# One late block of a factorisation-machine tower added on VectorE before the last layer-1 product, its sums copied earlier, and other shares for the last two steps

## The chip, the cores and the metric

The kernel runs on one core of one Trainium2 chip. The metric is the device time of one execution in microseconds (us), the median of the runs. One core has five engines with queues of their own: TensorE (PE in the profile, with PEld for its weight loads), VectorE (DVE), ScalarE (ACT), GpSimd (POOL) and SyncE (SP), which here only issues DMAs. They are held in step by semaphores: an instruction waits until a counter that others raise has reached a number.

## The reference, cut to what matters

```python
e = stack([tbl_f[ids[:, f]] for f in range(32)], axis=1)     # 2048 x 32 x 64, fp32
p, q = e[:, ROW_IDX], e[:, COL_IDX]                          # the 496 pairs of 32 fields
z = einsum('bne,hne,bnh->bn', p, kernel, q)                  # 2048 x 496
h = concatenate([z, dense_ctx], axis=1)                      # 2048 x 512
h = maximum(h @ W_top1 + b_top1, 0.0)                        # 512
h = maximum(h @ W_top2 + b_top2, 0.0)                        # 256
y = h @ W_top3                                               # 2048 x 1
```

## The kernel before

The batch of 2048 is cut into 8 pairs (`PAIRS`) of two times 128 rows, and each pair goes through 64 steps (`NS`), 512 steps (`STEPS`) in all. A step computes the products of one half slot, up to 16 field pairs for 128 rows (upright steps) or for 256 (turned steps): TensorE multiplies embeddings by the pair matrices into a ring of three PSUM tiles `T` (lines 730 and 742), and VectorE multiplies the result by the other embeddings (lines 586 and 604 to 612). For a turned step TensorE then sums over the partitions with a matrix of ones into `psZ` (line 767), several steps to a burst. For an upright step the 16 sums over 64 elements are divided: the first `share(n)` columns are summed by VectorE (line 633, with one instruction for two steps where that is possible) and the others by ScalarE, one column per instruction pair (line 523, an activation with an accumulator and the read of the accumulator). These sums land in `z` and are transposed on TensorE into the same `psZ` (line 681). Then ScalarE copies `psZ` to `zT` (line 510, `evacuate_z`, two of the four blocks of 128 features at once), and the dense layers run on it between the steps of the next pair.

The order on every engine is written out in advance by tables of steps. The last pair has no next pair, so its layers run in a tail after step 511. The change is in this tail and in the two steps ahead of it. In the kernel before:

- The last two steps, 510 and 511 (n = 62 and 63 of the last pair), are upright; `DVE_SHARE` gives VectorE 11 of the 16 columns of each and ScalarE 5. Their columns belong to the fourth block of z (k = 3) and so do those of a few steps before.
- ScalarE makes the sums of step 510, then the last copy of `psZ` (`evacuate_z(PASSES - 1)`, at `STEPS - 2`, line 510: blocks k = 2 and 3), and then the sums of step 511. The copy holds block 2 whole, but of block 3 only the sums of the turned steps: the upright sums are not ready when it is made.
- TensorE (lines 790 to 813) multiplies blocks 0 and 1 by W1 for the four groups m of 128 outputs (line 788), waits for the copy (`z_block_out`), multiplies blocks 2 and 3 of the copy, waits for all sums (`mult_done`, `dve_reduced`, `act_reduced`), and transposes the upright part of block 3 to PSUM (`LAST_Z`, line 808).
- ScalarE copies `LAST_Z` to `late` in SBUF (line 565). TensorE waits for that (`tail_act` 1), and multiplies `late` by the same weights of block 3 (line 812). So block 3 is multiplied twice, once for each part.
- The layer-1 results are added to the bias and cut at zero by ScalarE for m = 0 and 2 (line 568) and by VectorE for m = 1 and 3 (line 652), layer 2 follows (line 819), then its two ReLUs (lines 570 and 652), layer 3 (line 691), a copy to `y` (line 573) and the store (line 405).

An fp32 product of 128x128 weights with 256 columns is two matmul instructions in the profile.

Of the kernel before, what the change touches and what calls it, by code (L numbers as in the profile page):

```python
# [46 lines left out]
HALVED = (10, 14, 15, 16, 17, 19)  # L47
HALVED_FROM = 2
HALVED_LAST = (1, 2, 3, 5, 6, 7, 9, 10, 12, 15, 16, 17)
K_LEAD = 3  # L50
TR_STEP = (-12, -9, -1, 0, 6, 16, 29, 30)
TR_OUT = ((-15, 6), (-15, 6), (-4, 1), (-3, 5), (5, 2), (13, 3), (23, 8), (23, 8))
# [90 lines left out]
def dlrm_tower(nc, dense, ids, tables, W1, b1, W2, b2, W3, KT, out):  # L143
# [157 lines left out]
    with ctx:  # L301
# [54 lines left out]
        tail_dve = sem("tail_dve")  # L356
        y_out = [sem(f"y_out{u}") for u in range(2)]

        def share(n):

            return DVE_SHARE[ORDERED[n][0]]

        def embeddings(t, b, g):
            rows = slice(GF * (g % 2), GF * (g % 2) + GF)
# [4 lines left out]
        LAST_Z, L1_OUT = ends[4], (psE[:, 0:2 * P], ends[1], ends[2], ends[3])  # L369
        L2_OUT, L3_OUT = (ends[5], psZ[:, 0:2 * P]), ends[0]  # L370
        LAST_ZT = (PAIRS - 1) % 2
        late = zT[:, 1 - LAST_ZT, 0, :]

        FREE_AT = {}
        for t in range(1, PAIRS):
# [17 lines left out]
        @block.sync  # L393
        def _(sp):
            def load_k(s):
                sp.dma_start(kst[:, k_cols(s)], KT[:, k_cols(s)]).then_inc(k_in[s], 16)

            def load_dense(t):
                for b in (0, 1):
                    to = z[:, b, :].rearrange("p (b c) -> p b c", c=P)[:, :, P - DC // KC:P]  # L400
                    sp.dma_start(to, dense[bass.ts(2 * t + b, P), :].rearrange("p (b c) -> p b c", b=KC)).then_inc(dense_in, 16)

            def store_y(t):
                to = out[:, 2 * P * t:2 * P * (t + 1)].rearrange("o (q b) -> (o q) b", q=QUADS)
                sp.dma_start(to, y[0:P:QUAD, t % 2, :]).then_inc(y_out[t % 2], 16)

            sp.dma_start(idx[:, 0, :], ids[0:P, :]).then_inc(idx_first, 16)
            sp.dma_start(idx[:, 1, :], ids[P:2 * P, :]).then_inc(idx_second, 16)
            ready = {x: m for m, x in enumerate((x, b) for some, bs in UNITS[0] for x in some for b in bs)}
            loads = []  # L410
            for n in FIRST:
                s, x = ORDERED[n][0], max(ready[x] for part in stacks_of(n) for x in part)
                if s not in [load for load, _ in loads]:
                    loads.append((s, x))
            behind = {m: x for x, m in ready.items()}
            held = -1
            for m, (s, x) in enumerate(loads):
                if x - 2 * K_LEAD > held and x >= 2 * GS:
                    held = max(1, x - 2 * K_LEAD)
                    x, b = behind[held]  # L420
                    sp.wait_ge(gathered_0[b][x], 16 * 2)
                load_k(s)
                if m == 9:
                    sp.dma_start(idx[:, 2:2 * PAIRS, :], ids[2 * P:B, :].rearrange("(t p) f -> p t f", p=P)).then_inc(idx_rest, 16)
            sp.wait_ge(z_zero, 1)
            load_dense(0)
            some, bs = UNITS[0][-1]
            sp.wait_ge(gathered_0[bs[-1]][some[-1]], 16 * 2)
            sp.dma_start(w1[:, :, :], W1.rearrange("(k p) m -> p k m", p=P)).then_inc(weights_in, 16)
            sp.dma_start(w2[:, :, :], W2.rearrange("(k p) m -> p k m", p=P)).then_inc(weights_in, 16)  # L430
            sp.dma_start(w3[:, :], W3).then_inc(weights_in, 16)
            sp.dma_start(b1c[:, :], b1).then_inc(weights_in, 16)
            sp.dma_start(b2c[:, :], b2).then_inc(weights_in, 16)
            for t in range(PAIRS):
                if t > 0:
                    sp.wait_ge(bank_free, ordinal["l3", t - 1, 0] + 1)
                    store_y(t - 1)
                if t < PAIRS - 1:
                    sp.wait_ge(summed, 2 * bursts * (t + 1))
                    load_dense(t + 1)  # L440
            sp.wait_ge(tail_act, 5)
            store_y(PAIRS - 1)
            for u in range(2):
                sp.wait_ge(y_out[u], 16 * (PAIRS // 2))

        @block.gpsimd
        def _(pool):
            def gather(t, g, b, f):
                f += GF * g
                nc.gpsimd.indirect_dma_start(  # L450
                    out=embeddings(t, b, g)[:, f % GF, :], out_offset=None, in_=tables[f],
                    in_offset=bass.IndirectOffsetOnAxis(ap=idx[:, 2 * t + b, f:f + 1].bitcast(U32), axis=0),
                ).then_inc(gathered[b][g] if t else gathered_0[b][f // 2], 16)

            def halve(t, some):

                k, ring = share(some[0]), upright_at[t, some[0]] % SHARED_RING
                pool.wait_ge(mult_done, when(t, some[-1]) + 1)
                p = prod[:, ring:ring + len(some), 0:k * D].rearrange("p x (n h) -> p x n h", h=D)
                nc.gpsimd.tensor_tensor(p[:, :, :, 0:D // 2], p[:, :, :, 0:D // 2], p[:, :, :, D // 2:D], ALU.add).then_inc(half_done, 1)  # L460

            nc.gpsimd.memset(ident[:, :], 0.0).then_inc(ident_0, 1)
            pool.wait_ge(idx_first, 16)
            for m, (some, bs) in enumerate(UNITS[0]):
                for x in some:
                    for b in bs:
                        for f in (2 * x, 2 * x + 1):
                            gather(0, f // GF, b, f % GF)
                if m == 0:
                    assert bs == (0,)  # L470
                    pool.wait_ge(ident_0, 1)
                    nc.gpsimd.affine_select(out=ident[:, :], in_=ident[:, :], compare_op=ALU.not_equal, fill=1.0,
                                            base=0, pattern=[[-1, P]], channel_multiplier=1).then_inc(ident_1, 1)
                    pool.wait_ge(idx_second, 16)
            pool.wait_ge(idx_rest, 16)
            for t in range(PAIRS):
                for n in range(NS + 1):
                    if n < NS and GATHERS[t][n]:
                        if NS * t + n > 0:
                            pool.wait_ge(mult_done, NS * t + n)  # L480
                        gather(*GATHERS[t][n])
                    for some in REDUCES[t]:
                        if WHEN[t][some[-1]] == n - 1 and some[-1] in halved(t):
                            halve(t, some)

        @block.scalar
        def _(act):
# [24 lines left out]
            def reduce(t, n):  # L512
# [3 lines left out]
                    act.wait_ge(z_zero, 1)  # L516
                if (t, n) in FREE_AT:
                    act.wait_ge(summed, bursts * (2 * t - 1 + FREE_AT[t, n]))
                for k, m in enumerate(range(share(n), SIZE[s])):
                    if k > 0:  # L520
                        outs(when(t, n), k)
                    x = place(t, n)[:, m * D:(m + 1) * D]
                    last = nc.scalar.activation(x, x, ACT.Copy, accum_out=z[:, b, Z_COLUMNS[s][m]:Z_COLUMNS[s][m] + 1])  # L523
# [29 lines left out]
            for at in range(STEPS):  # L553
                t, n = at // NS, SEQ[at // NS][at % NS]
                outs(at, 0)
                if (t, n) in upright_at:
                    reduce(t, n)
                for m in range(1, 16):
                    outs(at, m)
                if at == STEPS - 2:  # L560
                    evacuate_z(PASSES - 1)
            assert not outs_at

            act.wait_ge(tail_pe, 1)
            nc.scalar.activation(late, LAST_Z, ACT.Copy).then_inc(tail_act, 1)
            for m in (0, 2):
                act.wait_ge(tail_pe, 2 + m)
                nc.scalar.activation(h1T[:, m, :], L1_OUT[m], ACT.Relu, bias=b1c[:, m:m + 1]).then_inc(tail_act, 1)
# [7 lines left out]
        def _(dve):  # L576
# [37 lines left out]
                last.then_inc(mult_done, 1)  # L614

            def reduce(t, some):
                k = share(some[0])
                ats = []
                for n in some:
                    s, b = ORDERED[n]  # L620
                    assert share(n) == k and Z_COLUMNS[s][:k] == list(range(Z_COLUMNS[s][0], Z_COLUMNS[s][0] + k))
                    ats.append(b * KC * P + Z_COLUMNS[s][0])
                by = ats[-1] - ats[0] if len(some) > 1 else P
                assert by != 0
# [26 lines left out]
            def relu(o, x, bias):  # L651
                nc.vector.tensor_scalar(o, x, bias, 0.0, ALU.add, ALU.max).then_inc(tail_dve, 1)

            for m in (1, 3):
                dve.wait_ge(tail_pe, 2 + m)
                relu(h1T[:, m, :], L1_OUT[m], b1c[:, m:m + 1])
# [4 lines left out]
        def _(pe):  # L661
# [137 lines left out]
                    last_l1(m, k, zT[:, LAST_ZT, k, :])  # L799
            pe.wait_ge(z_block_out, PASSES)  # L800
            for m in range(M1):
                for k in range(2, KC):
                    last_l1(m, k, zT[:, LAST_ZT, k, :])
            pe.wait_ge(mult_done, STEPS)
            pe.wait_ge(dve_reduced, reduces_of(NU * PAIRS))
            pe.wait_ge(act_reduced, NU * PAIRS)
            for b in (0, 1):
                last = nc.tensor.transpose(LAST_Z[:, b * P:(b + 1) * P], z[:, b, (KC - 1) * P:KC * P], ident[:, :])
            last.then_inc(tail_pe, 1)
            pe.wait_ge(tail_act, 1)  # L810
            for m in range(M1):
                last_l1(m, KC - 1, late).then_inc(tail_pe, 1)
            for k in range(M1):
                if k % 2:
                    pe.wait_ge(tail_dve, k // 2 + 1)
                else:
                    pe.wait_ge(tail_act, 2 + k // 2)
                for m in range(M2):
                    last = nc.tensor.matmul(L2_OUT[m], w2[:, k, m * P:(m + 1) * P], h1T[:, k, :], start=(k == 0), stop=(k == M1 - 1))
                    if k == M1 - 1:  # L820
                        last.then_inc(tail_pe, 1)
            for k in range(M2):
                if k:
                    pe.wait_ge(tail_dve, 3)
                else:
                    pe.wait_ge(tail_act, 4)
                for q in range(QUADS):
                    last = last_layer(L3_OUT, k, q)
            last.then_inc(tail_pe, 1)
# [43 lines left out]
```

## Time and profile before

| | us |
|---|---|
| median of 3 runs | 777.03 (776.97 to 777.16) |
| profiled execution, its own time | 776.94 |
| its span, first to last instruction | 775.0 |
| PE busy | 737.8 (95%) |
| DVE busy | 712.9 (92%) |
| ACT busy | 677.7 (87%) |
| POOL busy | 539.3 (70%) |

The rows are read like this: a start in us from the start of the span, a busy time in us, the engine, the line of the kernel, the operation, what it writes and reads, and how many instructions are merged in the row. A bracket behind a row is idle time of that engine just before it, with what ended it. Neighbouring instructions of one engine overlap a little in these rows, so the spacing of the starts, and not the duration, is what one more instruction costs in a full queue.

### The profile page before, as it was taken

Reading aid. Unit: us, or ns where it says so; the run is one execution under the profiler, and the core shown is the slowest. Engines: PE = TensorE matmul, PEld = TensorE weight load, DVE = VectorE, ACT = ScalarE, POOL = GpSimd, SP = SyncE. Lnnn points to the kernel's source line nnn. Section 1 sums busy time; section 2 is a strip of 40 time slices with the busy share of each in tenths; the row PEclk is TensorE's granted clock in tenths of the full one; section 3 lists DMA queues with packets and bytes.
Section 4 is the critical chain, followed back from the end, with each engine's and each line's share of the span. In section 5 each row is a group of like instructions: output and inputs, shape, how many; then the busy total and the mean of one; then the engine's idle time right before and its main releaser. Section 6 shows DMA issues by size and latency. Waiting matters only on the chain.

```text
span 775.0 us, 18419 instructions
## 1 busy us (share of the span) xinstructions
PE 737.8 (95%) x5448; PEld 447.9 (58%) x5448; DVE 712.9 (92%) x698; ACT 677.7 (87%) x5274; POOL 539.3 (70%) x560
## 2 busy tenths in 40 slices
PE   4589999899999999999999999999999999999998
PEld 1354545556546666666655666566756666556645
DVE  0679988989999999999999999999999999989993
ACT  1678986788898899998999999998999989998984
POOL 6777777777766678877787778877787777882110
PEclk9989999999999999999999999999999999999999
DMA  3345411111111111111111111111101111010000
GB/s 122 93 134 155 143 28 28 28 27 29 25 26 22 25 25 23 25 27 25 27 22 27 28 25 24 24 28 27 26 22 27 28 26 25 22 24 3 1 1 1
DMA packets 33187, 28.08 MB, mean 36 GB/s; under 512 B 19776, under 2 KB 20800, under 8 KB 33088
## 3 DMA queue, kind: packets, MB, share of 16 engines
q0 software_dynamic: 16384, 16.81, 9.7%
q1 hardware_dynamic: 16704, 10.11, 4.8%
q8 instruction: 43, 0.70, 0.4%
q14 instruction: 56, 0.46, 0.2%
HBM read 26.87 MB, written 0.01 MB: 35 GB/s over the span
## 4 chain that ended last, share of the span: by engine, by line
PE 79%; ACT 9%; DVE 5%; issue 4%; POOL 3%; DMA 0%; DVEq 0%; POOLq 0%
PE T L742 31%; PE T L730 19%; PE psZ L767 11%; PE psE L686 10%; ACT prod L523 7%; PE psE L671 4%; POOL E_low L450 3%; DVE prod L604 1%; DVE prod_t L586 1%; PE psZ L681 1%; ACT eT L494 1%; DVE z L633 1%; PE T L788 1%; DVE prod L607 0%; DVE prod L612 0%
## 5 line engine op out<-in xcount | busy, mean ns | idle before, releaser
L523 ACT ACTIVATE prod<-prod 128x64 f32<-128x64 f32 x2560 | 612.0, 246 | 14.6 <-DVE prod L604 6.1
L523 ACT ACTIVATION_READ_ACCUMULATOR prod<-prod 128x1 f32 x2560 | 493.9, 193 | 0.0
L742 PE MATMUL T<-kst,eT 64*128 64x512 f32 (+3 forms) x2304 | 329.8, 418 | 11.5 <-ACT eT L494 4.3
L450 POOL DMA_INDIRECT E_low<-tbl,idx x256 | 241.7, 944 | 86.3 <-issue 60.1
L450 POOL DMA_INDIRECT E_high<-tbl,idx x256 | 241.9, 945 | 81.7 <-issue 60.1
L604 DVE TENSOR_TENSOR prod<-T,E_low 128x1024 f32<-128x1024 f32 x192 | 229.6, 1215 | 27.4 <-DMA E_low<-tbl,idx 22.2
L586 DVE TENSOR_TENSOR prod_t<-T,eT 128x1024 f32<-128x1024 f32 x192 | 231.7, 1215 | 12.5 <-PE psZ L767 5.6
L742 PEld LDWEIGHTS T<-kst,eT 64*128 64x128 f32 x2304 | 178.6, 190 | 93.0 <-issue 41.2
L730 PE MATMUL T<-eT,kst 64*128 64x256 f32 x1536 | 202.7, 388 | 4.3 <-issue 1.7
L730 PEld LDWEIGHTS T<-eT,kst 64*128 64x128 f32 x1536 | 141.3, 187 | 78.1 <-issue 32.8
L633 DVE TENSOR_REDUCE z<-prod 128x16 f32<-128x1024 f32 (+18 forms) x179 | 154.2, 871 | 1.0 <-POOL prod L460 1.0
L494 ACT ACTIVATE eT<-psE 128x512 f32<-128x512 f32 (+2 forms) x83 | 41.0, 494 | 70.6 <-PE psE L671 70.4
L767 PE MATMUL psZ<-prod_t,ones 128*32 128x512 f32 x768 | 100.7, 597 | 0.0
L460 POOL TENSOR_TENSOR prod<-prod 128x640 f32<-128x640 f32 (+7 forms) x42 | 55.0, 1309 | 42.9 <-DVE prod L604 21.7
L686 PE MATMUL psE<-zT,w 128*128 128x256 f32 x224 | 55.8, 392 | 0.0
L686 PEld LDWEIGHTS psE<-zT,w 128*128 128x128 f32 x224 | 40.2, 189 | 18.0 <-issue 13.7
L767 PEld LDWEIGHTS psZ<-prod_t,ones 128*32 128x32 f32 x768 | 22.3, 109 | 46.9 <-issue 45.0
L607 DVE TENSOR_TENSOR prod<-T,E_low 128x1024 f32<-128x1024 f32 x32 | 38.7, 1213 | 3.0 <-PE T L742 3.0
L671 PE MATMUL psE<-ident,E_low 128*128 128x128 f32 x128 | 24.6, 300 | 17.1 <-DMA E_low<-tbl,idx 14.8
L607 DVE TENSOR_TENSOR prod<-T,E_high 128x1024 f32<-128x1024 f32 x32 | 38.7, 1213 | 0.9 <-PE T L742 0.9
L671 PEld LDWEIGHTS psE<-ident,E_low 128*128 128x128 f32 x128 | 14.3, 143 | 42.2 <-issue 29.6
L612 DVE TENSOR_TENSOR prod<-T,E_low 128x768 f32<-128x768 f32 x32 | 30.4, 950 | 3.6 <-PE T L742 3.6
(42 smaller groups left out, 198.7 us busy)
## 6 DMA issues: line engine op xcount, KB each, us to landing
kst<-K_T SPq DMA_DIRECT2D x28, 256.0 KB, 3.7
E_low<-tbl,idx POOLq DMA_INDIRECT x256, 2.4
E_high<-tbl,idx POOLq DMA_INDIRECT x256, 2.4
w<-W_top SPq DMA_DIRECT2D x1, 1024.0 KB
kst<-K_T SPq DMA_DIRECT2D x4, 192.0 KB, 2.4
w<-W_top SPq DMA_DIRECT2D x1, 512.0 KB
z<-dense_ctx SPq DMA_DIRECT2D x16, 8.0 KB
idx<-ids SPq DMA_DIRECT2D x1, 224.0 KB
```

Source lines behind the costliest of these rows:

```text
L450: nc.gpsimd.indirect_dma_start(out=embeddings(t, b, g)[:, f % GF, :], out_offset=None, in_=tables[f], in_offset=bass.IndirectOffsetOnAxis( ...
L460: nc.gpsimd.tensor_tensor(p[:, :, :, 0:D // 2], p[:, :, :, 0:D // 2], p[:, :, :, D // 2:D], ALU.add).then_inc(half_done, 1)
L523: last = nc.scalar.activation(x, x, ACT.Copy, accum_out=z[:, b, Z_COLUMNS[s][m]:Z_COLUMNS[s][m] + 1])
L586: nc.vector.tensor_tensor(place_turned(t, n).rearrange("p (q b) -> p q b", b=2 * P), T[:, s_ring(t, n), :].rearrange("p (q b) -> p q b", b ...
L604: last = nc.vector.tensor_tensor(p, ts, right.unsqueeze(1).broadcast_to([P, 2, GF, D]), ALU.mult)
L607: last = nc.vector.tensor_tensor(place(t, n).rearrange("p (k m) -> p k m", k=4), T[:, s_ring(t, n), :].rearrange("p (k m) -> p k m", k=4), ...
L633: nc.vector.tensor_reduce(bass.AP(to.tensor, to.offset, [list(to.ap[0]), [by, len(some)], [1, k]]), p, AX_X, ALU.add).then_inc(dve_reduced, 1)
L671: last = nc.tensor.transpose(psE[:, at * P:(at + 1) * P], embeddings(t, b, x // GS)[:, f:f + 2, :].rearrange("p f h -> p (f h)"), ident[:, :])
L686: last = nc.tensor.matmul(o, w(k), src[:, k, :], start=(k == 0), stop=(k == blocks - 1))
L730: last = nc.tensor.matmul(T[:, s_ring(t, n), x * BANK + y * 2 * P:x * BANK + (y + 1) * 2 * P], kst[rows, at + m * P:at + (m + 1) * P], eT[ ...
L742: last = nc.tensor.matmul(T[:, s_ring(t, n), bank + m * D:bank + (m + w) * D], eT[rows, i // 2, b * P:(b + 1) * P], kst[rows, at + m * D:a ...
L767: last = nc.tensor.matmul(psZ[quad * QUAD:(quad + 1) * QUAD, :], ones[:, QUAD - 2 - k // 2 * 2:2 * QUAD - 2 - k // 2 * 2], p[:, c * BANK:( ...
```

## The change

1. The last copy of `psZ` is issued by ScalarE ahead of the sums of step 510 and no longer behind them.
2. `LAST_SHARE` gives VectorE 14 of the 16 columns of steps 510 and 511, and ScalarE 2, in the last pair only.
3. TensorE multiplies only block 2 of the copy (`KC - 2`); the product of the copied part of block 3 is gone.
4. ScalarE's copy of `LAST_Z` to `late` is gone. In its place VectorE adds `LAST_Z` to block 3 of the copy, in place (`late` is now `zT[:, LAST_ZT, KC - 1, :]`), after waiting for the transposes (`tail_pe` 1) and the copy (`z_block_out`). TensorE waits for VectorE (`tail_dve` 1). The counts of `tail_act` and `tail_dve` in later waits are moved by one.

```diff
+LAST_SHARE = {62: 14, 63: 14}
...
-        def share(n):
+        def share(t, n):
 
-            return DVE_SHARE[ORDERED[n][0]]
+            return LAST_SHARE.get(n, DVE_SHARE[ORDERED[n][0]]) if t == PAIRS - 1 else DVE_SHARE[ORDERED[n][0]]
...
-        late = zT[:, 1 - LAST_ZT, 0, :]
+        late = zT[:, LAST_ZT, KC - 1, :]
...
-            sp.wait_ge(tail_act, 5)
+            sp.wait_ge(tail_act, 4)
...
                 outs(at, 0)
+                if at == STEPS - 2:
+                    evacuate_z(PASSES - 1)
                 if (t, n) in upright_at:
                     reduce(t, n)
                 for m in range(1, 16):
                     outs(at, m)
-                if at == STEPS - 2:
-                    evacuate_z(PASSES - 1)
...
-            act.wait_ge(tail_pe, 1)
-            nc.scalar.activation(late, LAST_Z, ACT.Copy).then_inc(tail_act, 1)
...
+            dve.wait_ge(tail_pe, 1)
+            dve.wait_ge(z_block_out, PASSES)
+            nc.vector.tensor_tensor(late, LAST_Z, late, ALU.add).then_inc(tail_dve, 1)
             for m in (1, 3):
                 dve.wait_ge(tail_pe, 2 + m)
                 relu(h1T[:, m, :], L1_OUT[m], b1c[:, m:m + 1])
...
             pe.wait_ge(z_block_out, PASSES)
             for m in range(M1):
-                for k in range(2, KC):
-                    last_l1(m, k, zT[:, LAST_ZT, k, :])
+                last_l1(m, KC - 2, zT[:, LAST_ZT, KC - 2, :])
...
-            pe.wait_ge(tail_act, 1)
+            pe.wait_ge(tail_dve, 1)
             for m in range(M1):
                 last_l1(m, KC - 1, late).then_inc(tail_pe, 1)
```

## Rows read from the trace of the kernel before

**Rows 1.** The chain of waits, last part: start us, us, what.

```profile
757.64 0.86 PE psZ L767 x8
758.50 1.06 PE psE L788 x4
759.56 2.59 PE T L788 x12
762.15 0.86 PE psE L788 x4
763.01 2.59 PE T L788 x12
765.60 0.23 PE T L808 x2
765.84 0.02 issue
765.86 0.39 ACT zT L565
766.25 0.04 issue
766.29 0.70 PE psE L788 x2
766.99 1.29 PE T L788 x6
768.29 0.43 PE T L819 x2
...
771.78 0.49 DVE h2T L652
772.27 0.04 issue
```

**Rows 2.** The timeline of PE's weight loads in the tail.

```profile
761.82 0.79 PEld L788 LDWEIGHTS psE<-zT,w 128*128 128x128 f32 x4
762.63 2.56 PEld L788 LDWEIGHTS T<-zT,w 128*128 128x128 f32 x12
765.23 0.36 PEld L808 LDWEIGHTS T<-ident,z 128*128 128x128 f32 x2
```

**Rows 3.** The timeline of ACT: first sum of step 510, the copy, last sum.

```profile
760.00 0.24 ACT L523 ACTIVATE prod<-prod 128x64 f32<-128x64 f32 x1
...
761.20 0.57 ACT L510 ACTIVATE zT<-psZ 128x512 f32<-128x512 f32 x1
761.67 0.24 ACT L523 ACTIVATE prod<-prod 128x64 f32<-128x64 f32 x1
...
762.77 0.19 ACT L523 ACTIVATION_READ_ACCUMULATOR prod<-prod 128x1 f32 x1
```

**Rows 4.** The timeline of DVE in the tail.

```profile
758.19 1.21 DVE L604 TENSOR_TENSOR prod<-T,E_low 128x1024 f32<-128x1024 f32 x1
759.32 1.67 DVE L633 TENSOR_REDUCE z<-prod 128x11 f32<-128x704 f32 x2
767.46 0.48 DVE L652 TENSOR_SCALAR h1T<-T,b1c 128x256 f32<-128x256 f32 x1 [6.48 <-PE T L788]
```

**Rows 5.** Groups by line and shape, whole span: count, busy us, mean ns, idle before.

```profile
L604 DVE TENSOR_TENSOR prod<-T,E_low 128x1024 f32<-128x1024 f32 x192 | 229.6, 1215 | 27.4 <-DMA E_low<-tbl,idx 22.2 <-PE T L742 3.8
L612 DVE TENSOR_TENSOR prod<-T,E_high 128x768 f32<-128x768 f32 x32 | 29.6, 951 | 0.0
L633 DVE TENSOR_REDUCE z<-prod 128x14 f32<-128x896 f32 x12 | 12.9, 1074 | 0.0
L633 DVE TENSOR_REDUCE z<-prod 128x4 f32<-128x256 f32 x8 | 3.3, 407 | 0.0
L565 ACT ACTIVATE zT<-T 128x256 f32<-128x256 f32 x1 | 0.4, 383 | 2.9 <-PE T L808 2.9
```

**Rows 6.** Stretches of the span: the clock granted to PE is the number behind POOL's.

```profile
0.00:40.00 40.00, 18.85 (x86) 9.66 (x86) 15.33 (x19) 14.50 (x97) 28.87 (x36) 0.99 0.39 106
...
762.00:766.00 4.00, 3.82 (x19) 3.12 (x18) 0.00 (x0) 1.10 (x10) 0.00 (x0) 1.00 0.00 0
766.00:770.00 4.00, 3.71 (x17) 3.29 (x18) 0.97 (x2) 1.19 (x3) 0.00 (x0) 1.00 0.00 0
```

More of the change, by code:

```diff
@@ L455, in halve @@
             def halve(t, some):
-                k, ring = share(some[0]), upright_at[t, some[0]] % SHARED_RING
+                k, ring = share(t, some[0]), upright_at[t, some[0]] % SHARED_RING
                 pool.wait_ge(mult_done, when(t, some[-1]) + 1)
@@ L518, in reduce @@
                     act.wait_ge(summed, bursts * (2 * t - 1 + FREE_AT[t, n]))
-                for k, m in enumerate(range(share(n), SIZE[s])):
+                for k, m in enumerate(range(share(t, n), SIZE[s])):
                     if k > 0:
@@ L616, in reduce @@
             def reduce(t, some):
-                k = share(some[0])
+                k = share(t, some[0])
                 ats = []
@@ L620, in reduce @@
                     s, b = ORDERED[n]
-                    assert share(n) == k and Z_COLUMNS[s][:k] == list(range(Z_COLUMNS[s][0], Z_COLUMNS[s][0] + k))
+                    assert share(t, n) == k and Z_COLUMNS[s][:k] == list(range(Z_COLUMNS[s][0], Z_COLUMNS[s][0] + k))
                     ats.append(b * KC * P + Z_COLUMNS[s][0])
@@ L814, in _ @@
                 if k % 2:
-                    pe.wait_ge(tail_dve, k // 2 + 1)
+                    pe.wait_ge(tail_dve, k // 2 + 2)
                 else:
-                    pe.wait_ge(tail_act, 2 + k // 2)
+                    pe.wait_ge(tail_act, 1 + k // 2)
                 for m in range(M2):
@@ L823, in _ @@
                 if k:
-                    pe.wait_ge(tail_dve, 3)
+                    pe.wait_ge(tail_dve, 4)
                 else:
-                    pe.wait_ge(tail_act, 4)
+                    pe.wait_ge(tail_act, 3)
                 for q in range(QUADS):
```

## The prediction, made before the changed kernel was run

> **What bounds the kernel now.** The profile's table of busy time puts TensorE first, but a share of the whole span says nothing of a change that touches only the last 15 us, so I went straight to the end of the chain of waits [rows 1]. There nearly everything is TensorE. From 758.50 to 765.60 it runs the layer-1 products of line 788 with no gap: 16 instructions for blocks 0 and 1, then at 762.15 another 16 for blocks 2 and 3. Then come the two transposes (line 808), 0.39 for ScalarE's copy of them, and the second product of block 3 from 766.29 on. Nobody else stands in the chain before 765.86. So in this stretch a TensorE instruction taken away is worth its whole time, until the next-latest input of the transposes is met, and an instruction put in the place of ScalarE's copy costs its difference to that copy.
>
> Next I looked up when the other inputs are ready: the copy of psZ and ScalarE's sums in ScalarE's timeline [rows 3], VectorE's sums in its own [rows 4], and, in the timeline of the weight loads [rows 2], when TensorE wants them.
>
> **The product that goes (part 3 of the change).** In the chain 12 instructions of line 788 take 2.59, which is 0.216 for each; the next 4 take 0.86, the same [rows 1]. A product of one block for one m is two instructions, 0.43. The change drops block 3 of the copy for four m: 8 instructions, 8 x 0.216 = 1.73 us, all on the chain. The products that stay are the same size; their other order (block 2 for each m, without block 3 between) costs nothing, since the late products already go to another m every time at 1.29 for 6 instructions, 0.215 for each [rows 1].
>
> **The add that replaces the copy (part 4).** ScalarE's copy of 128x256 takes 0.383 [rows 5]. The trace has no VectorE addition of 256 columns, so I bound it. VectorE's TENSOR_TENSOR with one operand in PSUM, the same kinds of operands, takes 1.215 for 1024 columns and 0.951 for 768 [rows 5]: 0.264 for 256 columns, so 256 columns come to 0.951 - 2 x 0.264 = 0.423. A reduction that reads 256 columns takes 0.407 [rows 5], and the bias-and-ReLU of 256 columns from PSUM 0.48 [rows 4]. I take 0.42, since the line through the same operation is the nearest. Towards cheap I go to 0.38, ScalarE's own time (all rows of VectorE for 256 columns lie above it, which excludes a gain); towards dear to twice the reduction, 0.81, as if the second operand were read by itself. The hand-overs stay: from TensorE to ScalarE 0.02 and back 0.04, and from VectorE to TensorE at 772.27 also 0.04 [rows 1]. So the swap costs 0.42 - 0.38 = 0.04, with bounds 0 and 0.43.
>
> The row shows VectorE at 0.423 against ScalarE at 0.383 for the same 256 columns. The Trainium skill has a rule that speaks against the swap: in "VectorE: DVE Perf Modes", section "Specifications", ScalarE sits closer to PSUM and VectorE closer to SBUF, and under "The TRN2 errata" a read from PSUM is 120 + N cycles at 0.96 GHz on VectorE, while an fp32 tensor_tensor is (N + 151)/0.96 ns. By these the add would be an estimated 0.39 or 0.42 us, and the sum would be 1.73 less 0.01 to 0.04; the trace agrees on 1024 columns within 0.01 (1.224 by the page, 1.215 measured).
>
> The add's new wait for the transposes stands on VectorE's queue, and behind it are the ReLUs for m = 1 and 3. They wait for products that come after the add in any case, and VectorE had been idle for 6.48 us ahead of them [rows 4]. Its second wait, for the copy, is met 4 us before. ScalarE loses an instruction there and keeps its ReLUs for m = 0 and 2, which wait for TensorE as before. No DMA moves; SyncE's wait is only renumbered, and GpSimd has nothing to do in the tail.
>
> **The copy moved ahead (part 1).** ScalarE reaches step 510 at 760.00 and gives the copy 0.47 of its queue (761.20 to the next start at 761.67) [rows 3]. Moved ahead, the copy ends at 760.57 instead of 761.77. It has nothing to wait for there: the last burst of sums on TensorE (line 767) was over at 758.50 [rows 1]. TensorE wants the copy at 761.82, where its weight loads for blocks 2 and 3 begin [rows 2], and its matmuls run on without a gap [rows 1]. So before, the copy was in time by 0.05, and the earlier copy saves nothing in this profile: 0, with the limit that if the unprofiled runs sometimes miss those 0.05 they gain some tenths at most, say one sum of ScalarE, 0.24. What it delays is ScalarE's sums of step 510, by 0.47; the end of all sums stays where it was.
>
> **The shares (part 2).** ScalarE's last sum ended at 762.96, TensorE began to load for the transposes at 765.23 [rows 2, 3]. With 1.73 less on TensorE it wants them at 763.50, so with the old shares 0.54 would still be left, and the shares are worth 0 as well. With the new ones ScalarE ends at 760.00 + 0.47 + 4 x 0.24 + 0.09 = 761.52. VectorE's two reductions grow from 704 to 896 elements, 1.07 each [rows 5]; two of 704 took 1.67 from 759.32 [rows 4], so two of 896 take about 2.07 and end at 761.39. Both leave 2 us of slack to 763.50. This slack is the cover: were the sums later than 763.50, every microsecond would be paid in full.
>
> **The sum.** Block 3's product -1.73, the swap +0.04, copy and shares 0: -1.69. The transposes end at 764.11, the add runs from 764.13 to 764.55, the late products start at 764.59 instead of 766.29, and from there on nothing changes: the same 8 instructions, layer 2, the ReLU, layer 3, the store. On the profiled execution's own time: 776.94 - 1.69 = 775.25, with a span of 773.3; from the median of 777.03 it is 775.34. Forecast: **775.3**. With the bounds of the add this is 775.3 to 775.7.
>
> **The rivals.**
> *The gain is there but under the mark.* A difference of about 0.2%, 1.55 us here, is what a measurement of this kernel can tell from no change, and the forecast of 1.69 is over it by 0.14 only. An add at 0.56 or more, a slower hand-over to VectorE after its idle stretch, or a shift of the other 760 us by as much as the three runs differ among themselves (0.19) would each do. For: there is no row of this add, and the margin is small. Against: three different rows of VectorE come to 0.41 to 0.48. Time: 775.7 (at the dear bound, 776.94 - 1.73 + 0.43 = 775.64, or 775.73 from the median).
>
> *The sums become the last wait.* The transposes wait for VectorE's wider reductions or ScalarE's sums. It decides from 763.50 on. I get 761.5 for both; the reductions would have to take 2.1 each instead of 1.07. If they ended 1 us late, 776.3. Against: twelve reductions of this very shape have a mean of 1.074 [rows 5].
>
> *The earlier copy also pays.* If TensorE misses the copy in ordinary runs, 0.24 to 0.4 come on top: 775.0. For: 0.05 of slack. Against: the profiled run, whose own time is that of the others within 0.1, shows no gap.
>
> *Slower: TensorE's clock.* It is at full speed, 1.00, that is 2.4 GHz, throughout the tail [rows 6]. If the pause for the add, or the lower load after it, let it fall to its other level of 1.2 GHz at 764.1, the 24 instructions after it (8 of line 788, and 16 of layer 2 in eight rows like the one at 768.29 [rows 1]) would take 5.2 us more, and layer 3 0.3: 775.3 + 5.5 = 780.8. It decides from a pause that is long enough to cost the clock. For: in the first 40 us, with TensorE busy for under half, the granted clock was under full, 0.99 [rows 6]. Against: the pause of 0.45 before (765.84 to 766.29) left it at 1.00, and mine is 0.48. The Trainium skill ("TensorE: Matmul & The Clock Gate", section "What's actually happening") says that the throttled state is the default and activity lifts it; the trace agrees in so far as the busy tail keeps 1.00.
>
> **How the numbers follow.** Forecast with the add at 0.38 to 0.5: 0.55. The earlier copy pays too: 0.08. Gain under the mark: 0.29. Sums last: 0.05, within 0.2% as well. Clock: 0.03. That gives faster 0.63, the same 0.34, slower 0.03. The range of 8 in 10 goes from 774.9 (the copy pays, 775.0, less the spread of runs) to 775.9 (the dear bound of the add, 775.73, and the spread of runs above it, 0.19).
>
> **What would show it.** After: 8 instructions fewer in line 788 (32 instead of 40), no gap in the chain up to the transposes, which end near 764.1; a VectorE TENSOR_TENSOR of 256 columns at about 0.42, where ScalarE's copy was; the copy at 760.0 with an end at 760.6; last reduction at 761.4, last ScalarE sum at 761.5; everything after it 1.69 sooner. The prediction is wrong if a gap opens before the transposes, the add takes over 0.56, the clock is under 1.00 in the tail, or steps far from the tail shift.

## The result and the profile after

| | before | after |
|---|---|---|
| median, us | 776.94 (775.89 to 777.27, 10 runs) | 775.28 (774.08 to 775.68, 10 runs) |
| ratio, 95% interval | | 0.9977 (0.9968 to 0.9985) |
| span of the profiled execution | 775.0 | 773.6 |
| tail: end of the last burst into psZ to end of the copy to y | 14.40 | 12.71 |

The kernel is faster by 1.66 us in the medians (0.21%); the ratio puts it at 0.23%, with an interval from 0.15 to 0.32%. So the gain is clear of zero, but whether it is more than 0.2% is not decided. The tail in the last row is read from the chain of waits, from the start of line 788 (790 in the changed kernel), to the end of the copy to `y`: 758.50 to 772.90 before, 758.82 to 771.53 after. It is 1.69 shorter. The two spans differ by only 1.4, since this execution of the changed kernel came to its tail 0.32 later. That difference arises in the first 59 us and has nothing to do with the change (last section). I compare tails from here on.

The chain of waits of the changed kernel, last part (start us, us, what), stands against [rows 1]:

```profile
758.82 1.06 PE psE L790 x4
759.88 2.59 PE T L790 x12
762.47 0.43 PE psE L790 x2
762.90 1.29 PE T L790 x6
764.19 0.23 PE T L809 x2
764.42 0.02 issue
764.45 0.43 DVE zT L655
764.88 0.04 issue
764.93 0.70 PE psE L790 x2
765.63 1.29 PE T L790 x6
766.92 0.43 PE T L820 x2
```

The second batch of line 790, for block 2 alone, is 8 instructions and takes 1.72, where [rows 1] had 16 and 3.45. There is no gap between it and the transposes. VectorE stands where ScalarE stood, with 0.43 for 0.39 in this view, and the hand-overs are 0.02 and 0.04 as before.

The timeline of VectorE (DVE) in the changed kernel, against [rows 4]:

```profile
758.50 1.21 DVE L603 TENSOR_TENSOR prod<-T,E_low 128x1024 f32<-128x1024 f32 x1
759.63 2.07 DVE L632 TENSOR_REDUCE z<-prod 128x14 f32<-128x896 f32 x2
764.45 0.42 DVE L655 TENSOR_TENSOR zT<-T,zT 128x256 f32<-128x256 f32 x1 [2.75 <-PE T L809]
```

The timelines of ScalarE and of TensorE's weight loads, against [rows 3] and [rows 2]:

```profile
760.32 0.58 ACT L511 ACTIVATE zT<-psZ 128x512 f32<-128x512 f32 x1
...
761.66 0.19 ACT L524 ACTIVATION_READ_ACCUMULATOR prod<-prod 128x1 f32 x1
```

```profile
762.09 0.41 PEld L790 LDWEIGHTS psE<-zT,w 128*128 128x128 f32 x2
...
763.82 0.36 PEld L809 LDWEIGHTS T<-ident,z 128*128 128x128 f32 x2
```

The copy ends at 760.90, 1.2 ahead of the loads for block 2. The sums end at 761.70 on VectorE and 761.85 on ScalarE, 2.0 ahead of the loads for the transposes at 763.82.

The row of the add in the groups by line and shape (count, busy us, mean ns, idle before), against the last of [rows 5]:

```profile
L655 DVE TENSOR_TENSOR zT<-T,zT 128x256 f32<-128x256 f32 x1 | 0.4, 425 | 2.7 <-PE T L809 2.7
```

### The profile page after: what moved, and what is told of

Same layout as the page of the kernel before. It is cut to its first block, busy times and chain, and to the rows that moved or that the text cites. A ratio compares the mean times of both kernels' runs of the same rounds, so it can differ in the third digit from the quotient of the medians.

```text
span 773.6 us, 18392 instructions
## 1 busy us (share of the span) xinstructions
PE 739.6 (96%) x5440; PEld 449.1 (58%) x5440; DVE 713.9 (92%) x699; ACT 676.1 (87%) x5261; POOL 539.4 (70%) x560
## 4 chain that ended last, share of the span: by engine, by line
PE 79%; ACT 9%; DVE 5%; issue 4%; POOL 3%; DMA 0%; DVEq 0%; POOLq 0%
PE T L744 31%; PE T L732 19%; PE psZ L769 11%; PE psE L688 10%; ACT prod L524 7%; PE psE L673 4%; POOL E_low L451 3%; DVE prod L603 1%; DVE prod_t L585 1%; PE psZ L683 1%; ACT eT L495 1%; DVE z L632 1%; PE T L790 1%; DVE prod L606 0%; DVE prod L611 0%
```

## The experiments

Every run is compared by its tail, since single executions of one kernel differ by more than a microsecond: the kernel before, measured anew with each set of runs, had medians of 776.94, 776.26, 777.02 and 776.69. Where the last burst doesn't stand in the chain (e6, e9, e10), its end is taken 0.07 behind the first weight load of line 790, as in the others. The times are given for completeness; those of one run say nothing of a difference this small.

| run | what is different | tail, us | time, us |
|---|---|---|---|
| before | | 14.40 | 776.94 |
| after | | 12.71 | 775.28 |
| e1_old_shares | after, VectorE's share back at 11 | 12.71 | 774.81 (1 run) |
| e2_old_copy | after, copy behind the sums of step 510 | 12.71 | 774.29 (1 run) |
| e3_product_alone | after, old shares and old place of the copy | 12.72 | 774.76, ratio 0.9979 (0.9969 to 0.9988) |
| e4_shares_copy_alone | before, new shares and early copy | 14.40 | 776.19, ratio 1.0001 (0.9992 to 1.0011) |
| e5_add_twice | after, the add issued twice | 13.06 | 775.68 (1 run) |
| e7_scalar_copy | after, ScalarE's copy for the add, copied sums of block 3 left out | 12.67 | 774.57 (1 run) |
| e10_share_9 | after, VectorE's share 9 | 13.10 | 775.63 (1 run) |
| e6_share_5 | after, VectorE's share 5 | 16.57 | 779.59 (1 run) |
| e8_transposes_first | after, transposes ahead of block 2 | 11.93 | 773.84, ratio 0.9960 (0.9947 to 0.9974) |
| e9_first_old_shares | the same with the old shares | 13.09 | 775.44 (1 run) |
| e11_after_again | after, once more | 12.72 | 775.28, ratio 0.9979 (0.9970 to 0.9988) |
| e12_first_again | e8 once more, same chip as e11 | 11.93 | 774.15, ratio 0.9969 (0.9957 to 0.9981) |

### Which part carries the gain

The theory is the prediction's: the dropped product is the whole gain, shares and copy give slack that nobody uses. Its rival is that the earlier copy or the shares carry a part of it. The changed kernel without its new shares:

```diff
-LAST_SHARE = {62: 14, 63: 14}
+LAST_SHARE = {}
```

> The changed kernel with VectorE's share of the last two steps back at 11 of 16 (ScalarE 5). The tail is measured from the end of the last burst of sums to the end of the copy to y: 14.40 us in the trace of before (758.50 to 772.90), 12.71 in that of after (758.82 to 771.53). My theory (the shares only add slack): ScalarE makes 6 more sums of 0.24, its last one ends 1.44 later, about 2.7 us after the last burst instead of 3.0 less the rest, that is near 763.3 on the clock of after, still ahead of the 763.82 at which TensorE loads the transposes; tail 12.7. Rival (sums become the last wait without the new shares): the transposes start late and the tail is 13.0 or more.

The tail is 12.71. ScalarE's last sum ended at 762.55, and TensorE began to load for the transposes at 763.08: 0.53 of slack are left, 0.54 had been forecast. (The "about 2.7 us" in the expectation is a slip: 3.03 and 1.44 make 4.47 us after the burst, which is what the 763.3 beside it says, and 4.47 is what was measured.)

```profile
762.35 0.20 ACT L524 ACTIVATION_READ_ACCUMULATOR prod<-prod 128x1 f32 x1
```

```profile
763.08 0.35 PEld L809 LDWEIGHTS T<-ident,z 128*128 128x128 f32 x2
```

Next, the copy in its old place:

```diff
                 outs(at, 0)
-                if at == STEPS - 2:
-                    evacuate_z(PASSES - 1)
                 if (t, n) in upright_at:
                     reduce(t, n)
                 for m in range(1, 16):
                     outs(at, m)
+                if at == STEPS - 2:
+                    evacuate_z(PASSES - 1)
```

> The changed kernel with the last copy of psZ back behind ScalarE's sums of step 510 (which are 2 now). My theory: the copy ends 0.5 us later than in after, about 761.4, ahead of the 762.1 at which TensorE loads the weights of block 2; tail 12.7, as after. Rival (the earlier copy pays by itself): tail longer by 0.2 to 0.4, 12.9 to 13.1.

The tail is 12.71 again. Both of these edits together leave the dropped product and the add:

> Only the dropped product and the add on VectorE; old shares, old place of the copy. My theory: the copy ends as in before, some 0.05 before TensorE wants it, the sums end about 0.5 before the transposes; the whole gain is here: tail 12.7 to 12.8, 1.6 to 1.7 us under before. Rival (shares and copy carry part of the gain): tail 13.0 to 13.5, gain 1.2 or less.

The tail is 12.72 and the ratio 0.9979, that of the changed kernel. In its timelines of ScalarE and of the weight loads the copy is in time by as little as in [rows 2, 3]:

```profile
761.39 0.57 ACT L511 ACTIVATE zT<-psZ 128x512 f32<-128x512 f32 x1
```

```profile
762.01 0.36 PEld L790 LDWEIGHTS psE<-zT,w 128*128 128x128 f32 x2
```

It ended at 761.96 and the load began at 762.01, 0.05 later, but the matmuls behind it ran without a gap. The other way round, the kernel before with parts 1 and 2 of the change (the early copy and the new shares) and nothing else:

> The kernel before with only the new shares and the earlier copy; block 3 is still multiplied twice and ScalarE still copies the transposes. My theory: no change, tail 14.4, time within 0.1% of before. Rival (the earlier copy pays too): tail 14.0 to 14.2.

The tail is 14.40 and the ratio 1.0001. So the rival falls: the product and the swap are the whole gain, and the two other parts are worth nothing where they stand.

This run also shows how the copy was "in time by 0.05". The weight loads of the kernel before, and then of this run, where the copy had been over for more than a microsecond:

```profile
759.18 2.56 PEld L788 LDWEIGHTS T<-zT,w 128*128 128x128 f32 x12
761.82 0.79 PEld L788 LDWEIGHTS psE<-zT,w 128*128 128x128 f32 x4
```

```profile
757.93 2.56 PEld L789 LDWEIGHTS T<-zT,w 128*128 128x128 f32 x12
760.52 0.84 PEld L789 LDWEIGHTS psE<-zT,w 128*128 128x128 f32 x4
```

Here the next load began 0.03 behind the load before it, in the kernel before 0.08 behind, and in e3 0.07. So the load was held up by the late copy, by 0.04 or 0.05, and those 0.05 between the end of the copy and the load look like the hand-over (0.02 to 0.04 elsewhere in this tail) and not like slack. It cost nothing because the loads run ahead of their matmuls: 761.82 against 762.15. How much later the copy could have come wasn't tried.

### What the add costs

```diff
+            nc.vector.tensor_tensor(zT[:, 1 - LAST_ZT, 0, :], LAST_Z, late, ALU.add)
             nc.vector.tensor_tensor(late, LAST_Z, late, ALU.add).then_inc(tail_dve, 1)
```

> The changed kernel with the add issued twice on VectorE, the first time into a tile that nobody reads. Theory (the add lies whole on the path, 0.42 for one): the tail, 12.71 in after, becomes 13.05 to 13.15. Rival (the add is covered, the gap of 0.51 on TensorE is mostly hand-over): 12.8 or less.

The tail grew by 0.35, to 13.06. The chain of waits has the two adds one behind the other, and so has the timeline of VectorE:

```profile
764.25 0.42 DVE zT L655
764.68 0.34 DVE zT L656
```

```profile
764.25 0.42 DVE L655 TENSOR_TENSOR zT<-T,zT 128x256 f32<-128x256 f32 x1 [2.75 <-PE T L810]
764.59 0.42 DVE L656 TENSOR_TENSOR zT<-T,zT 128x256 f32<-128x256 f32 x1
```

The add is on the path. A second one costs 0.34 and not 0.42, because it starts 0.34 behind the first one, before that has ended. Other neighbouring VectorE rows do the same: in [rows 4] a multiplication of 1.21 is followed after 1.13.

In the next run ScalarE copies the transposes to a tile of its own, as before, and TensorE multiplies that alone. The copied sums of block 3 are left out of layer 1, so this kernel computes less than the reference and serves only to price a step. Without the renumbered counts of later waits:

```diff
-        late = zT[:, LAST_ZT, KC - 1, :]
+        late = zT[:, 1 - LAST_ZT, 0, :]
...
+            act.wait_ge(tail_pe, 1)
+            nc.scalar.activation(late, LAST_Z, ACT.Copy).then_inc(tail_act, 1)
...
-            dve.wait_ge(tail_pe, 1)
-            dve.wait_ge(z_block_out, PASSES)
-            nc.vector.tensor_tensor(late, LAST_Z, late, ALU.add).then_inc(tail_dve, 1)
...
-            pe.wait_ge(tail_dve, 1)
+            pe.wait_ge(tail_act, 1)
```

> The changed kernel with ScalarE's copy of the transposes in the place of VectorE's add; the copied sums of block 3 are left out of layer 1, to price the swap by itself. Theory: the copy takes 0.38 against 0.42 for the add, the hand-overs are the same: tail 12.67. Rival (waking VectorE after 2.75 us of idle time costs more than waking ScalarE, so the swap cost more than the difference of the two durations): 12.6 or less.

12.67, so the swap costs 0.04, the difference of the durations (0.425 and 0.383), and VectorE's 2.75 of idle time in front of the add cost nothing that shows at 0.01. The chain has ScalarE's copy where the add was:

```profile
763.51 0.39 ACT zT L566
```

The same run isolates the other term. Against the kernel before it lacks the product of the copied block 3 and has parts 1 and 2, which e4 showed to be worth nothing; its tail is 1.73 shorter than 14.40. That is the price of the dropped product.

### Where the slack of the sums ends

```diff
-LAST_SHARE = {62: 14, 63: 14}
+LAST_SHARE = {62: 5, 63: 5}
```

> The changed kernel with VectorE's share of the last two steps at 5 of 16, so ScalarE makes 22 sums behind the copy. In after the copy starts 1.50 us after the last burst of psZ. The prediction says that the slack of the sums covers them up to the point where TensorE loads the transposes, 5.00 us after that burst, and that every us beyond is paid in full: last sum at 1.50 + 0.48 + 22 x 0.24 + 0.1 = 7.36, transposes 2.4 late, tail 12.71 + 2.4 = 15.1. Rival (late sums are partly absorbed, for instance by other work on TensorE): tail 13.5 to 14.5.

The tail is 16.57, 1.5 over the theory. The wait itself came out as expected: the transposes ended 7.89 after the burst, against 5.60 in the changed kernel, 2.29 late. But the four late products took 3.56 in place of 1.99 (0.70 and 1.29 in the changed kernel's chain). Parts of this run's chain of waits:

```profile
766.48 0.42 PE T L809 x2
...
767.40 1.22 PE psE L790 x2
768.62 2.34 PE T L790 x6
770.96 0.43 PE T L820 x2
```

Stretches of this run, with TensorE's granted clock as the number behind POOL's:

```profile
760.00:764.00 4.00, 4.00 (x20) 3.51 (x19) 0.69 (x2) 4.00 (x33) 0.00 (x0) 1.00 0.00 0
764.00:766.00 2.00, 0.38 (x2) 0.00 (x0) 0.00 (x0) 2.00 (x19) 0.00 (x0) 1.00 0.00 0
766.00:768.00 2.00, 1.01 (x4) 0.71 (x5) 0.42 (x1) 0.33 (x4) 0.00 (x0) 0.80 0.00 0
768.00:770.00 2.00, 2.00 (x6) 1.64 (x5) 0.48 (x1) 0.47 (x1) 0.00 (x0) 0.50 0.00 0
770.00:772.00 2.00, 2.00 (x9) 1.67 (x9) 0.48 (x1) 0.47 (x1) 0.00 (x0) 0.85 0.00 0
```

TensorE had been idle for 2.10 ahead of the transposes and 0.52 ahead of the late products, and then its clock stood at 0.50, that is 1.2 GHz, while it ran most of those products. Cut finer, it is 1.00 up to the end of the transposes (766.00 to 766.90), 0.79 in the pause for the add (766.90 to 767.40) and 0.50 in the first late product (767.40 to 768.62); from 770.96 on, in layer 2, it is 1.00 again. The pauses stand in TensorE's timeline:

```profile
766.48 0.41 PE L809 MATMUL T<-ident,z 128*128 128x128 f32 x2 [2.10 <-ACT prod L524]
767.40 1.22 PE L790 MATMUL psE<-zT,w 128*128 128x256 f32 x2 [0.52 <-DVE zT L655]
```

A shorter lateness tells the two prices apart:

```diff
-LAST_SHARE = {62: 14, 63: 14}
+LAST_SHARE = {62: 9, 63: 9}
```

> The changed kernel with VectorE's share of the last two steps at 9 of 16: ScalarE's last sum ends 1.50 + 0.48 + 14 x 0.24 + 0.1 = 5.44 us after the last burst, 0.4 to 0.5 behind the moment at which TensorE would load the transposes (5.00). Theory: the short lateness is paid as it is, with 0.2 for starting TensorE again, the clock stays at 1.00 in the tail: 13.0 to 13.2. Rival (any pause in front of the transposes costs the clock, as the share of 5 did, where the granted clock fell to 0.50 behind the pause): 14.3 or more.

The tail is 13.10. The last sum ended 5.42 after the burst (5.44 was expected), the transposes ended at 5.99, 0.39 later than in the changed kernel, and that is what the tail grew by. TensorE was idle for 0.19 ahead of the transposes, the transposes themselves took 0.42 in the chain in place of 0.23, and the clock stayed at 1.00:

```profile
764.08 0.41 PE L809 MATMUL T<-ident,z 128*128 128x128 f32 x2 [0.19 <-ACT prod L524]
765.00 0.70 PE L790 MATMUL psE<-zT,w 128*128 128x256 f32 x2 [0.52 <-DVE zT L655]
```

The short lateness was paid once; the long one of the share of 5 was paid once and then 1.57 more on the products behind it. Each is one run.

### A version with the pause filled

The pause of 0.51 on TensorE (764.42 to 764.93) is the add. Block 2 doesn't need it, so its products can run there:

```diff
-            pe.wait_ge(z_block_out, PASSES)
-            for m in range(M1):
-                last_l1(m, KC - 2, zT[:, LAST_ZT, KC - 2, :])
             pe.wait_ge(mult_done, STEPS)
             pe.wait_ge(dve_reduced, reduces_of(NU * PAIRS))
             pe.wait_ge(act_reduced, NU * PAIRS)
             for b in (0, 1):
                 last = nc.tensor.transpose(LAST_Z[:, b * P:(b + 1) * P], z[:, b, (KC - 1) * P:KC * P], ident[:, :])
             last.then_inc(tail_pe, 1)
+            pe.wait_ge(z_block_out, PASSES)
+            for m in range(M1):
+                last_l1(m, KC - 2, zT[:, LAST_ZT, KC - 2, :])
             pe.wait_ge(tail_dve, 1)
```

> The changed kernel with the transposes ahead of the products of block 2, so that TensorE multiplies block 2 (1.73 us) while VectorE adds. In after the sums are ready 3.03 us after the last burst (ScalarE) and 2.88 (VectorE), TensorE would want them at 3.27. Theory: no wait for the sums, the gap of 0.51 on TensorE goes: tail 12.2, about 0.5 us under after and 2.2 under before. Here the new shares would pay. Rival (the sums are too late at that place): a gap opens ahead of the transposes and eats the gain, tail 12.5 or more.

The tail is 11.93, 0.78 under the changed kernel and more than the 0.5 that I had expected. Its chain of waits:

```profile
758.97 2.59 PE T L790 x12
761.56 0.22 PE T L806 x2
761.77 0.43 PE psE L790 x2
762.21 1.29 PE T L790 x6
763.50 0.43 PE psE L790 x2
763.94 1.29 PE T L790 x6
```

The first late product (763.50) takes 0.43 here, and 0.70 behind the pause in the changed kernel. The pause cost 0.51 and 0.27 for starting again, and my theory had left out the 0.27. A likely reason for it, which no run isolates, is the weight load: the changed kernel's first late load begins at 764.93 together with its product, while in this run that load begins at 763.13, 0.37 ahead of it.

With the old shares of 11 and 5 in this order:

> The kernel with the transposes first (tail 11.93, the transposes' weights loaded 3.27 us after the last burst), with the old shares of 11 and 5. With those, in the run with old shares alone, ScalarE's last sum ended 4.47 us after the burst. Theory: here the shares are on the path; the transposes come 1.2 to 1.3 late, block 2 behind them too, tail 13.1 to 13.5. Rival (the shares stay worth nothing): 11.9 to 12.0.

13.09. The transposes ended 5.03 after the burst in place of 3.86, 1.17 late, and the tail grew by 1.16. TensorE was idle for 0.96 ahead of them, and the clock stayed at 1.00:

```profile
762.95 0.41 PE L806 MATMUL T<-ident,z 128*128 128x128 f32 x2 [0.96 <-ACT prod L524]
```

Here the new shares carry weight that they don't have in the changed kernel. Then both orders side by side on one chip:

> The changed kernel once more, unchanged, beside the next one on the same chip. Theory: ratio 0.997 to 0.999 to the kernel before, tail 12.71, wherever the start of the kernel puts the whole. Rival (the gain of 0.23% hung on the chip or on the start): ratio 0.999 or more.

> The kernel with the transposes first once more, beside the changed kernel on the same chip. Theory: its tail is 11.93 and the time is 0.8 us (0.1%) under the changed kernel and 2.47 us under before, ratio 0.9968. Rival (the earlier run's 0.996 was a lucky start): no difference to the changed kernel.

The tails are 12.72 and 11.93, the medians 775.28 (11 runs) and 774.15 (6 runs), the ratios to the kernel before 0.9979 and 0.9969. The intervals of the two ratios overlap; the difference of 0.79 is shown by the tails, twice each, and not by these ratios alone.

## Why the prediction was right

The forecast was 775.3 and the median is 775.28, the gain forecast 1.69 and measured 1.66 in the medians, 1.69 in the tail. The tail is the test of the mechanism, and there the agreement holds term by term. That the two absolute times agree within 0.02 is luck: the forecast started from a median of three runs, and the median of the kernel before moved between 776.26 and 777.02 from set to set; against its own set, the second measurement of the changed kernel (e11) is 1.41 below in the medians.

- **The dropped product, -1.73.** Right: 1.72 for the 8 instructions that stay, where 16 took 3.45, and 1.73 by e7's tail.
- **The swap, +0.04.** Right: 0.425 in its row of the groups. The forecast's 0.423 came from the line through 768 and 1024 columns; no row showed it, though one sentence of the prediction says so. e7 priced the swap at 0.04. By the formula for an fp32 tensor_tensor in the Trainium skill ("VectorE: DVE Perf Modes", "The TRN2 errata") such an add is an estimated 0.424, and the trace agrees; the 120 + N cycles for a read from PSUM in the same section, an estimated 0.39, do not fit. That ScalarE sits closer to PSUM (the Trainium skill, "VectorE: DVE Perf Modes", "Specifications") agrees in sign with the 0.04 for 256 columns, but a copy and an add are not the same operation, so this is weak support.
- **The earlier copy, 0.** Right (e2, e4), but the reason was misread: the 0.05 was a hand-over and not slack, and what covered it was the lead of the weight loads. That the copy might pay 0.24 in ordinary runs stays open as far as the ratios go, since 0.24 is 0.03% and the intervals of e3 and e4 reach 0.1%; the chains of the kernel before and of e3, both with the copy late, show no gap.
- **The shares, 0.** Right (e1, e4), with the forecast slack of 0.54 measured as 0.53. The new slack of 2 us was right too.
- **The sums as the last wait.** It did not come about, but e10 and e6 showed the point from which it decides where I had put it. "Every microsecond would be paid in full" was wrong in size: e6 paid 3.86 for a lateness of 2.29, while e10 (0.39 for 0.39) and e9 (1.16 for 1.17) paid what it says.
- **TensorE's clock.** Not here: 1.00 throughout the tail of the changed kernel. e6 shows that the mechanism is real in this tail, with a pause of 2.10 and one of 0.52 close together; with the 0.51 of the changed kernel alone the clock stayed at 1.00. My price of 5.5 supposed that the clock stays down to the end; e6 paid 1.57, since it was back at full speed in layer 2.
- **The spread of runs.** This step was wrong. I took 0.19 from three runs. Ten runs of before reach from 775.89 to 777.27 and ten of after from 774.08 to 775.68, so 4 of those 10 lie under my range of 774.9 to 775.9, though the median doesn't. The chance of a gain clear of 0.2% should have been nearer to one half: the interval of the ratio includes 0.998. And "steps far from the tail shift", which the prediction names as a sign of being wrong, did come about (0.32 at the start of the tail), but runs of the same work shift as much among themselves.

## What to carry to other kernels

When a sum is linear, add the late part to the early part before the product rather than multiply both: on a chain of TensorE work it pays the whole product, less what the add takes more than the copy it replaces. Ahead of such a change, list when each other input of the next step is ready; edits that only widen a slack give nothing until another edit, here the order of e8, uses it. And look at what an engine does while it waits for the added step: filling that pause was worth half as much again as the change itself.

## What the runs showed of the hardware that was not expected

**The spread arises before 59 us, most of it behind 24 us.** VectorE begins its first pair of multiplications between 24.26 and 24.68 us in the 14 profiles. A later pair, which it begins at 58.86 in the kernel before, comes at 57.56 in e4 and at 59.34 in e6, the earliest and the latest. From this pair to the start of the tail it is 699.61 to 699.70 in all 14 profiles. So these 700 us of the kernel repeat within 0.1.

What it comes from is less clear. The granted clock in the stretch from 40 to 50 us differs too. In the profiles of e4 and of the changed kernel:

```profile
40.00:50.00 10.00, 8.75 (x56) 5.47 (x57) 7.94 (x8) 7.53 (x58) 7.56 (x9) 0.83 0.45 130
```

```profile
40.00:50.00 10.00, 9.07 (x48) 5.98 (x47) 7.24 (x8) 5.94 (x46) 7.56 (x9) 0.64 0.45 129
```

| clock granted, 40 to 50 us | start of the tail, us |
|---|---|
| 0.83 (e4, e2) | 757.25, 757.53 |
| 0.77 to 0.79 (e1, e7, e8, e11) | 757.53 to 758.08 |
| 0.68 to 0.70 (before, e3, e5, e9, e10) | 758.33 to 758.69 |
| 0.64 to 0.66 (after, e6, e12) | 758.80 to 759.00 |

All these kernels do the same work up to step 509. The spread of 1.7 us in the last column is of the size of the spread of the times. In this one stretch clock and start go together, but the stretch was chosen after the fact, and in the one before it, 30 to 40 us, they do not: there the clock was 0.96 in the kernel before and 0.70 in e11, which came to its tail 0.97 sooner. That the clock is the cause is not shown.

**Restarting TensorE costs more than the pause.** Two instructions of an fp32 product of 256 columns took 0.43 in a running stream and 0.70 behind a pause of 0.5, two transposes 0.23 and 0.42 (e10, behind 0.19), and a filled pause gave back 0.78 for 0.51 (e8).

**A pause can be paid for afterwards.** After pauses of 2.10 and 0.52 TensorE ran most of the eight instructions of the late products at half clock (e6, 1.57 more than at full clock); after one of 0.19 and one of 0.52 it did not (e10), nor after one of 0.96 (e9). One run each.
